# One transfer per part for the first four units' rows, and projections of two chunks moved into the first attention

## What is computed

```
mod = silu(c) @ wmod                       # six rows of 256: sa, ca, ga, sb, cb, gb
ga, gb = sign * max(|.|, 0.25)
h = layernorm(x) * (1 + ca) + sa
x = x + ga * attention(h)
h = layernorm(x) * (1 + cb) + sb
x = x + gb * ffn(h)
```

## Time and profile before

| what | us |
|---|---|
| median of three runs | 1556.82 |
| lowest, highest | 1551.09, 1563.71 |
| the profiled execution | 1552.29 |
| its span, first to last instruction | 1550.6 |
| mean granted TensorE clock in it | 0.972 of full |

### The profile page before, as it was taken

How to read it: one execution, slowest core, us unless ns; L and a number is a source line. 1 busy time by engine, 2 the same in 40 slices (tenths; PEclk the granted TensorE clock), 3 DMA queues, 4 the chain that set the end, 5 groups by cost and what they waited for, 6 DMA issues and landing times.

```text
span 1550.6 us, 35254 instructions
## 1 busy us (share of the span) xinstructions
PE 1404.3 (91%) x13320; PEld 593.6 (38%) x13320; DVE 1199.2 (77%) x1592; ACT 1038.3 (67%) x2052; POOL 316.9 (20%) x376
## 2 busy tenths in 40 slices
PE   7887888899899999986899999999999989999998
PEld 5543333333333254442233333333333333236665
DVE  5678797898786044888899979997999779816766
ACT  2245575777688833231798978998988879984443
POOL 2401132000000033223500018200400040046225
PEclk9989999999999999996899999999999999999999
DMA  7621121111000003222200200000000000012455
GB/s 227 128 56 41 50 67 34 31 28 49 5 2 2 1 15 65 53 48 51 93 7 7 54 6 7 7 7 7 7 7 7 7 2 2 2 62 84 142 152 149
DMA packets 57611, 68.54 MB, mean 44 GB/s; under 512 B 10563, under 2 KB 53123, under 8 KB 56707
## 3 DMA queue, kind: packets, MB, share of 16 engines
q1 hardware_dynamic: 54379, 57.90, 14.1%
q0 software_dynamic: 3072, 8.39, 1.8%
HBM read 45.29 MB, written 26.74 MB: 46 GB/s over the span
## 4 chain that ended last, share of the span: by engine, by line
issue 40%; PE 32%; DVE 11%; POOL 8%; ACT 4%; DMA 3%; SPq 2%; POOLq 0%; DVEq 0%; ACTq 0%
DVE mpart L1747 8%; PE psum L1235 7%; PE psum L1210 4%; PE psum L1278 3%; PE psum L1179 3%; ACT probs L1482 3%; PE psum L1287 3%; PE psum L1306 3%; PE psum L1352 2%; PE psum L1371 1%; POOL ffn_w L953 1%; PE psum L1139 1%; DMA key_region<-in_w_up 1%; POOL key_region L965 1%; SPq L803 1%
## 5 line engine op out<-in xcount | busy, mean ns | idle before, releaser
L1747 DVE TENSOR_REDUCE mpart<-psum 128x2 f32<-128x1024 f32 (+2 forms) x832 | 913.7, 1155 | 101.4 <-PE psum L1179 84.3
L1482 ACT ACTIVATE probs<-psum 128x512 f32<-128x512 f32 (+3 forms) x1664 | 846.1, 573 | 172.1 <-PE psum L1210 94.9
L1235 PE MATMUL psum<-probs,v_region 128*17 128x256 f32 (+2 forms) x6144 | 495.2, 395 | 11.6 <-ACT out_sb L1497 7.9
L1179 PE MATMUL psum<-key_region,row_region 50*128 50x512 f16 (+3 forms) x1664 | 320.8, 378 | 65.9 <-DVE mpart L1747 50.6
L1210 PE MATMUL psum<-row_region,key_region 52*128 52x512 f16 (+3 forms) x1664 | 349.7, 378 | 15.7 <-ACT probs L1482 12.9
L1210 PEld LDWEIGHTS psum<-row_region,key_region 52*128 52x128 f16 x1664 | 97.8, 93 | 352.9 <-ACT probs L1482 292.1
L1235 PEld LDWEIGHTS psum<-probs,v_region 128*17 128x17 f32 x6144 | 102.7, 95 | 205.1 <-issue 101.1
L1179 PEld LDWEIGHTS psum<-key_region,row_region 50*128 50x128 f16 x1664 | 94.5, 93 | 167.5 <-DVE mpart L1747 98.1
L909 POOL TENSOR_SCALAR vare<-mv 128x4 f32<-128x4 f32 x16 | 3.7, 230 | 637.1 <-DVE mv L1661 637.1
L1517 ACT ACTIVATE probs<-psum,gate_s 128x512 f32<-128x512 f32 (+1 forms) x24 | 16.4, 682 | 69.8 <-PE psum L1278 69.8
L1018 POOL TENSOR_TENSOR key_region<-probs,key_region 128x512 f16<-128x512 f32 (+1 forms) x24 | 27.9, 1164 | 155.4 <-ACT key_region L1526 155.3
(11 more groups left out here) (191 smaller groups left out, 1329.2 us busy)
## 6 DMA issues: line engine op xcount, KB each, us to landing
parts<-key_region SPq DMA_DIRECT2D x32, 256.0 KB, 2.6
key_region<-parts SPq DMA_DIRECT2D x48, 128.0 KB, 4.5
row_region<-parts SPq DMA_DIRECT2D x192, 32.0 KB
sorted_x<-in_zero SPq DMA_DIRECT2D x46, 128.0 KB, 2.6
key_region<-sorted_x SPq DMA_DIRECT2D x46, 128.0 KB, 2.3
sorted_y<-key_region SPq DMA_DIRECT2D x46, 128.0 KB
key_region<-in_wmod SPq DMA_DIRECT2D x2, 1536.0 KB, 11.4
x_sb<-in_x SPq DMA_DIRECT2D x4, 512.0 KB, 8.7
```

Of the source, the lines that this page charges most:

```text
L1179: mm = pe.matmul(bank(b + par)[:, 0:w], rows[at, g, hp, r * P:(r + 1) * P], keys[at, g * HP + hp, q * CH:q * CH + w], start=True, stop=not ...
L1235: mm = pe.matmul(psum[32 * h:32 * h + VW, SUM_BANK, lo:hi], v_sb[:, jt, g * HG + h, :], probs[:, (S0[y] + s) % 2, h, lo:hi], start=(jt == ...
L1482: nc.scalar.activation(probs[:, (S0[y] + s) % 2, 2 * hp + par, off:CH], psum[:, e % 3, off:CH], ACT.Exp, scale=SCALES[y]).then_inc(s_p, 1)
L1747: V.tensor_reduce(mpart[:, n % NG, at:at + 2, q:q + 1], psum[:, b:b + 2, 0:w], AX.X, ALU.max).then_inc(drained(*item)[0], 1)
```

## The change

1. **Rows.** The rows of units 0 to 3 are loaded by one item, with one transfer per part and half: six of 128 KB instead of 24 of 32 KB. For layer 0 the two constant transfers (16 KB each) go among the first loads, for layer 1 they stand ahead of the six. The rows of chunk 0 have a semaphore of their own. One constant that nothing used (`identb`) is dropped.
2. **Projections.** `qk`, `v` and `keys` of chunks 2 and 3, the gates of layer 1 (`mg`, `gates`) and the router's rows (`mr`) leave the prologue and are put between the steps of units 0 to 3. VectorE's part of each (`ql`, `va`, `gates`, `ra`) stands behind the next slot item.
3. **Order in the prologue.** The gates of layer 0 come after six blocks instead of ahead of the first projection; the blocks of unit 0 start behind the second projection of chunk 1; V's matmuls and their sum on VectorE are separate items. `mc` of layer 1 comes after the placing of unit 0.
4. **Memory.** The silu of c and the gates' scratch move from the buffer of the probabilities to the end of a weight buffer, so the first exponentials wait for no gates.

```diff
 def prologue_walk():
     early = prologue_blocks()
-    out = [("cv",), ("st", 0, 0), ("nm", 0, 0), ("ln", 0, 0), ("mc", 0), ("st", 0, 1), ("ws",), ("mg", 0), ("nm", 0, 1), ("st", 0, 2)]
-    out += [("qk", 0, 0, 0), ("ql", 0, 0, 0), ("ln", 0, 1), ("lh", 0, 1), ("qk", 0, 0, 1), ("ql", 0, 0, 1), ("keys", 0, 0), ("gates", 0), ("v", 0, 0), ("nm", 0, 2)]
-    out += [("st", 0, 3), ("rows", 0, 0), ("rows", 0, 1), ("rows", 0, 2), ("rows", 0, 3)]
-    out += [("qk", 0, 1, 0), ("ql", 0, 1, 0), ("ln", 0, 2), ("lh", 0, 2), ("qk", 0, 1, 1), ("ql", 0, 1, 1), ("keys", 0, 1), ("v", 0, 1), ("nm", 0, 3)]
-    out += [("mc", 1), ("mg", 1), ("mr",), ("wo", 0), ("xb", 0, 0), ("xb", 0, 1), ("xb", 0, 2)]
-    for it in (("qk", 0, 2, 0), ("ql", 0, 2, 0), ("ln", 0, 3), ("lh", 0, 3), ("xb", 0, 3), ("qk", 0, 2, 1), ("ql", 0, 2, 1), ("keys", 0, 2), ("v", 0, 2)):
-        out += [it] + [early.pop(0) for _ in range(2 * (it[0] in ("ql", "lh", "v")))]
-    out += [("mp", 0, 0), ("gates", 1), ("qk", 0, 3, 0), ("ql", 0, 3, 0), early.pop(0), early.pop(0), ("mt", 0, 0), ("place", 0, 0)]
-    out += [("qk", 0, 3, 1), ("ql", 0, 3, 1), ("keys", 0, 3), early.pop(0), early.pop(0), ("v", 0, 3)]
+    out = [("cv",), ("st", 0, 0), ("nm", 0, 0), ("ln", 0, 0), ("mc", 0), ("sh", 0), ("st", 0, 1), ("ws",), ("nm", 0, 1), ("st", 0, 2)]
+    out += [("qk", 0, 0, 0), ("ql", 0, 0, 0), ("ln", 0, 1), ("lh", 0, 1), ("qk", 0, 0, 1), ("ql", 0, 0, 1), ("keys", 0, 0), ("rows", 0, 0)]
+    out += [("v", 0, 0), ("nm", 0, 2), ("va", 0, 0), ("st", 0, 3), ("qk", 0, 1, 0), ("ql", 0, 1, 0), ("ln", 0, 2), ("lh", 0, 2), ("nm", 0, 3)]
+    out += [("qk", 0, 1, 1), ("ql", 0, 1, 1), early.pop(0), early.pop(0), ("ln", 0, 3), ("lh", 0, 3), early.pop(0), early.pop(0)]
+    out += [("v", 0, 1), early.pop(0), early.pop(0), ("keys", 0, 1), ("va", 0, 1), ("mg", 0), early.pop(0), early.pop(0), ("mp", 0, 0), ("gates", 0)]
+    out += [early.pop(0), early.pop(0), ("mt", 0, 0), ("place", 0, 0), ("mc", 1), early.pop(0), ("sh", 1)]
+    out += [("wo", 0), ("xb", 0, 0), ("xb", 0, 1), ("xb", 0, 2), ("xb", 0, 3)]
     return out + early
+
+def with_projections(items):
+    after = {(0, 0): [("qk", 0, 2, 0)], (0, 2): [("qk", 0, 2, 1)], (1, 0): [("v", 0, 2)], (1, 1): [("keys", 0, 2)], (1, 2): [("mg", 1)],
+             (1, 3): [("qk", 0, 3, 0)], (2, 1): [("qk", 0, 3, 1)], (2, 2): [("v", 0, 3)], (3, 0): [("keys", 0, 3)], (3, 1): [("mr",)]}
+    part = {"qk": "ql", "v": "va", "mg": "gates", "mr": "ra"}
+    out, left, step = [], [], None
+    for it in items:
+        if it[0] == "sc" and it[5] == 0:
+            out += after.get(step, [])
+            left += [(part[e[0]], *e[1:]) for e in after.get(step, []) if e[0] in part]
+            step = it[3:5]
+        out.append(it)
+        if it[0] in IN_SLOT and left:
+            out += left
+            left = []
+    return out
...
         if p == 0:
-            out.extend([("rows", 1, n) for n in range(NG)])
+            out.append(("rows", 1, 0))
...
+            def first_row_constants(y):
+                for par in range(2):
+                    sp.dma_start(rows[64 * par:64 * par + C0, :, :, :].rearrange("p g h t -> p (g h) t"),
+                                 a[f"row_const{y}"][:, :, 0:CH]).then_inc(s_rows, 16)
+
+            def load_first_rows(y):
+                sp.wait_ge(*parts_stored(y, 0, 0))
+                if y:
+                    first_row_constants(y)
+                for par in range(2):
+                    for k, part in enumerate(ROW_PARTS):
+                        src = parts[0, part, :, 0:CH].rearrange("(h r c) t -> r c h t", r=2, c=HD)[par]
+                        lo = 64 * par + C0 + HD * k
+                        sp.dma_start(rows[lo:lo + HD, :, :, :].rearrange("p g h t -> p (g h) t"), src).then_inc(s_rows, 16)
...
-                if s == 0 and y == 0 and hp == 0:
-                    act.wait_ge(s_mod, NLAY)
```

More of the change, by code:

```diff
@@ L540, in adaln_two_layers @@
             "p (h k n) -> p h k n", h=2, k=KD) for i in range(3)]
-        prob_words = probs[:, :, :, :].rearrange("p b h t -> p (b h t)")
-        csb = prob_words[:, 0:2 * KD * P].rearrange("p (k n) -> p k n", k=2 * KD)
-        gtmp = prob_words[:, 2 * KD * P:2 * KD * P + 4 * D].rearrange("p (k n) -> p k n", k=2)
+        first_end = ffn_w[:, 0, KD * F0:]
+        csb = first_end[:, 0:2 * KD * P].rearrange("p (k n) -> p k n", k=2 * KD)
+        gtmp = first_end[:, 2 * KD * P:2 * KD * P + 4 * D].rearrange("p (k n) -> p k n", k=2)
         sil = [probs[:, 0, b, :] for b in range(2)]
@@ L643, in adaln_two_layers @@
         s_key = [sem(f"keys_loaded{q}") for q in range(NCH)]
+        s_rows = sem("first_chunk_rows_loaded")
         s_row = [sem(f"rows_loaded{g}") for g in range(NG)]
@@ L708, in rows_loaded @@
         def rows_loaded(y, n):
-            i = n // NG
-            return 128 * (i + 1) if y == 0 else 128 * NCH + 128 + 96 * i
+            i, g = n // NG, n % NG
+            if i == 0:
+                return s_rows, 128 * (y + 1)
+            return s_row[g], 128 * i if y == 0 else 128 * (NCH - 1) + 96 * i
         def parts_stored(y, tc, side):
@@ L839, in _ @@
                 sp.dma_start(keys[64 * par + M0:64 * par + KS, :, :], a["col_max"]).then_inc(s_kc, 16)
+            first_row_constants(0)
             load_wmod(1)
-            for dst, name in ((identh, "identh"), (identb, "identb"), (gate_s, "gate_s"), (up_s, "up_s")):
+            for dst, name in ((identh, "identh"), (gate_s, "gate_s"), (up_s, "up_s")):
                 sp.dma_start(dst[:, :], a[name]).then_inc(s_const, 16)
@@ L853, in _ @@
                     load_keys(*it[1:])
+                elif it[0] == "rows" and it[2] == 0:
+                    load_first_rows(it[1])
                 elif it[0] == "rows":
@@ L946, in split_ffn @@
                 else:
-                    pool.wait_ge(s_const, 16 * 12)
+                    pool.wait_ge(s_const, 16 * 11)
                     link(nc.gpsimd.tensor_copy(gate_w16[:, 0, :, :], gate_w[:, :, :]))
@@ L1171, in max_pair @@
                 b = open_slot(item)
-                pe.wait_ge(s_row[g], rows_loaded(y, n))
+                pe.wait_ge(*rows_loaded(y, n))
                 pe.wait_ge(s_key[q], 96 * (y + 1))
@@ L1388, in _ @@
                     if it[1:3] == (0, 0) and it[3:] == (0, 0, 0):
-                        pe.wait_ge(s_const, 16 * 12)
+                        pe.wait_ge(s_const, 16 * 11)
                     max_pair(it)
@@ L1625, in shift_rows @@
                 V.tensor_copy(brow[:, 1, :], bank(bank_of(item))[:, D:2 * D]).then_inc(drained(*item)[0], 1)
-            def raw_gates(item):
-                dve.wait_ge(*filled(*item))
-                V.tensor_copy(gab[:, item[1], :], bank(bank_of(item))).then_inc(drained(*item)[0], 1)
             def gates(y):
                 g = gab[:, y, :]
+                dve.wait_ge(*filled("mg", y))
+                V.tensor_copy(g, bank(bank_of(("mg", y)))).then_inc(drained("mg", y)[0], 1)
                 dve.wait_ge(*drained("mg", y))
@@ L1895, in _ @@
                     silu_of_c()
-                elif it[0] == "mc":
-                    shifts(it)
-                elif it[0] == "mg":
-                    raw_gates(it)
+                elif it[0] == "sh":
+                    shifts(("mc", it[1]))
                 elif it[0] == "gates":
@@ L1911, in _ @@
                     low_parts(("qk", *it[1:]))
-                elif it[0] == "v":
-                    value(it)
+                elif it[0] == "va" or it[0] == "v" and it[1]:
+                    value(("v", *it[1:]))
                 elif it[0] == "max":
@@ L1927, in _ @@
                     low_hidden(it)
-                elif it[0] == "mr":
-                    shift_rows(it)
+                elif it[0] == "ra":
+                    shift_rows(("mr",))
                 elif it[0] == "rt":
@@ L1953, in constants @@
     col_max[0] = BIG
-    row0 = np.ones((C0, HP, T), np.float16)
+    row0 = np.ones((C0, NG * HP, T), np.float16)
     row0[1] = -far * t
```

14 lines of the change are left out of this document (6 added, 8 removed).

## The result

The changed kernel is slower: 1589.35 us (median of four runs, 1587.00 to 1593.05) against 1557.57 (1551.09 to 1563.71) for the kernel before, a ratio of 1.0191 [1.0159, 1.0222]. Ratios in this text, with 95% intervals, are those on record for the runs taken together; they differ a little from the quotient of the two medians, here 1.0204. The forecast was 1558 with a range up to 1574, so the time lies outside it. The profiled execution took 1588.48 us for a span of 1586.6, which is 36.0 more than the span of before. Over the whole span little can be seen, and that row answers to the earlier trace rows: 17 us more of TensorE, and a lower share.

A forecast was written before the change was run, and what follows sets the result against it. It saw slack ahead of the attention, partly from SP's row transfers, and hardly any in units 4 to 6. Terms -15.1 + 13.5 + 2.5 = +0.9 us gave 1558; own range 1550 to 1566, 8 in 10 from 1545 to 1574.

The forecast's parts named there:

- Units 0 to 3: First attention units: the moved work, priced with TensorE up to 0.93 busy and VectorE 0.91, costs +13.5 us.
- With the dense projections I take the clock as full: Unit 0: added projections lift TensorE's clock, so its 3.4 us lost to the lower clock vanish; unit cost +2.0.
- The trace agrees in units 0 and 1: Claim that activity releases the throttle: clock 0.76 and 0.88 while TensorE waits for VectorE, 1.00 in units 2 and 3.
- The second rival: Units 0 to 3: projections hold bank pairs and ScalarE waits in order, +34.6 us there, 1579 in all; chance 0.15.
- TensorE and VectorE each idle some 10 us here: Units 0 to 3: reason for staying near the lower end, +7.7, rather than the upper, +34.6.
- Ahead of the attention: Prologue: rows land at 47, first scores come at 71.2 instead of 86.3, so 15.1 us earlier.
- the bound of 48.4: Prologue: late end for the rows' landing, twelve transfers of 1.57 MB taking 12.8 us at 123 GB/s.
- The estimate by the Trainium skill: Prologue: 2.3 us per 128 KB transfer, so rows land at 43, forecast 4 us lower; the trace's 4.5 was used.
- The third rival: Prologue gives less: rows at 48.4, lower clock, first scores at 78.3 (-8.0); +9 in all, 1566; chance 0.15.
- What bounds: Opening reading: slack ahead of the attention, some from SP's 32 row transfers delaying a store ScalarE awaits for 15.7 us.
- Layer 1: Feed-forward stage: the wait for unit 0's rows ends at 613.9 instead of 611.3, +2.5 us, between 0 and +3.5.
- The signs named for a wrong forecast: Unit 4 before 130 or after 148, first scores after 76, or later time differing over 3 us beyond layer 1's rows.

The follow-up runs named there:

- a0_changed: The changed kernel as it is, run again on another chip beside the kernel before; ratio to before 1.0186, units 0 to 3 in 92.18 us.
- e10: Kernel before with layer 0's rows grouped, layer 1's gates after the prologue's last block, and six bursts of 13 zero-weight matmuls in units 0 to 2; ratio 1.0004.
- e11: Kernel before with layer 0's rows grouped, layer 1's gates after the prologue's last block, and six bursts of two VectorE operations in units 0 to 2; ratio 0.9992.
- e3: Changed kernel with 4 of 12 matmuls in the moved projections and 8 of 24 in the moved V; VectorE's work whole; ratio to before 1.0060.
- e4: Changed kernel with high and low parts of the moved projections written for 32 of 512 columns, all matmuls made; ratio to before 1.0128.
- e9: Changed kernel with both the matmul cut of e3 and the column cut of e4; ratio to before 1.0050.
- e7: Changed kernel with each moved item behind the step's second pair of scores instead of ahead of the first; ratio to before 1.0169.
- e1: Kernel before with only the rows of units 0 to 3 grouped into one item, both layers; projections stay in the prologue; ratio 0.9989.
- e2: Changed kernel with eight row transfers per unit as before, so the moves without the grouping; ratio to before 1.0120.

## Why the prediction was wrong

- **Units 0 to 3, the step that failed.** "Unit by unit, with TensorE at best 0.93 busy and VectorE 0.91" took the idle shares as room. It gave +13.5; measured were +41.0 and, in a0_changed, +36.9. The counts of the moved work were right: VectorE's busy time rose by 12.3, where the sum was 11.8. But the highest busy share nearby comes from units in which small pieces alternate on both engines (and 0.91 was not the highest for VectorE: the stretch that gave TensorE its 0.93 has VectorE at 18.06 of 19.00, or 0.95). With a piece of 3 to 5 us on TensorE, VectorE runs dry: 4.82 us in the changed kernel, 4.39 in e10. The added times then follow one another: 21.5 + 11.8 = 33.3. e10 shows it for TensorE's time alone, e11 for VectorE's with a lower clock in it, e3, e4 and e9 by taking the work away. That the cause is the reach of two bank pairs, about a block each, is my reading of the walk; no run had more pairs in this stage.
- **The remainder**, 3.6 to 7.7 us over 33.3, goes with the clock. "With the dense projections I take the clock as full" was wrong: 0.77 and 0.85 in the two profiles, against 0.91. TensorE's busy time rose by 33.9 and 27.6 for 21.5 us of added matmuls, so 12.4 and 6.1 of it are the lower clock's, not all on the path. How much of the remainder that is wasn't separated. e10's bursts, with no emptying, raised the clock (0.89 to 0.93), and e11's on VectorE lowered it (to 0.80). The Trainium skill ("TensorE: Matmul & The Clock Gate", "What's actually happening") makes activity release the throttle. These rows neither bear it out nor refute it: TensorE's busy share was 0.82 with and without the projections and the clock fell, but the same matmuls fill more time at the lower clock. "The trace agrees in units 0 and 1" was read from too little as well: by the earlier trace rows TensorE was busy 0.89 and 0.81 of those units, and 0.82 and 0.78 of units 2 and 3, where the clock was 1.00. The step from more matmuls to a full clock had no row behind it.
- **The second rival** had the price nearly right (+34.6 in the stage, 1579), by a cause that isn't needed. It named held bank pairs and ScalarE. e10 loses a microsecond for each one added without either, and e7, with ScalarE's order changed, loses the same as the change. What a held pair adds to that in the changed kernel no run separates. Its end was the full matmul time plus the emptying by ScalarE and VectorE, 21.5 + 13.1, close by its number to the series; I had dismissed it since "TensorE and VectorE each idle some 10 us here": the same error.
- **Ahead of the attention** -15.1 was forecast, and the first scores came 10.7 earlier. Of the 4.4 us that are missing, 3.5 are the landing of the rows and 0.8 the walk behind it. The rows landed at 50.5, not at 47 and not within the bound of 48.4: 4.5 us was the median of key transfers that mostly have no rows right behind them, and the throughput bound took 123 GB/s where 112 were had. The estimate by the Trainium skill ("DMA: Bandwidth & Descriptors", "Anatomy of one DMA") was 43; the trace disagrees still more than it did in the earlier trace rows. From there to the first scores the walk took 25.0 us where 24.2 were forecast. That it came so near is luck, since two errors nearly cancel. TensorE had the lower clock twice, behind the pause and again from 66 us on; I had counted only 2.2 us of work at it, behind the pause, and the columns alone lost 2.5 (6.14 instead of 3.63). Against that the fourteen blocks took some 6.2 us, from start to start in the timeline, where 8.4 were put down. The wait for the gates, 2.7 in the forecast and 3.02 in the trace, lies ahead of that second stretch. The third rival, first scores at 78.3, was nearer here.
- **What bounds** was read too hopefully: the store behind SP's rows looked like the cause of the slack, and e1 shows that undoing it is worth 1.2 us in the first scores. The gain of the prologue came from the 33 us of work on TensorE and VectorE that left it (e2, with the moves alone, has its first exponential 14.8 us earlier than before), and that work came back at its full price.
- **Layer 1**: the mechanism was right. +2.5 was forecast and +3.5 measured, and e2 without grouping has 3.60, the wait of before. The term of the earlier trace rows was too short by 1.0: 609.8 plus 4.5 is 614.3, not 613.9, so +3.0 by the prediction's own figures, and the rest is a landing of 4.9 instead of 4.5 and 0.15 more on SP.
- **Behind unit 3** nothing was forecast apart from layer 1's rows, and units 4 to 15 differ by 1.1 us. The signs named for a wrong forecast came: unit 4 after 148 (unit 3's sums were copied at 172.57).

## What to carry to other kernels

Where two engines hand small buffers to and fro, the idle share of each is the time in which it waits for the other, and no room for more work: price anything put between them at the sum of its times on both engines. More buffers, enough to cover the longest piece, may change that; no run here tried it. A burst on zero weights, or a few operations on scratch memory, measures this before the real work is moved. Group transfers only behind the one that somebody waits for, and before undoing a long wait look at what the engine that would do the released work is doing meanwhile.

## What was not expected of the hardware

- Transfers of 128 KB each, six behind six others, landed 8.5 us after the last was issued, against a median of 4.5 for the key transfers of the kernel before. In layer 1 the six rows' transfers, with two constants ahead, were issued by 641.55 and the wait ended at 646.42, 4.9 us later; unit 0's eight small ones were issued by 609.9 and the wait ended at 611.3.
- 32 float32 matmuls of one column each took 6.14 us in the changed kernel, from 66 us on at a granted clock of 0.50, and 3.63 at 1.00 in the kernel before: 192 against 113 ns each.
- The moved projections did not raise the granted clock: 0.91 without them, 0.77 and 0.85 with them, and 0.91 with projections and 52 fillers. Bursts of matmuls with nothing to empty raised it from 0.89 to 0.93, and added work on VectorE alone lowered it from 0.89 to 0.80.
